# Half of the short convolution of two state-space stages moved from VectorE to GpSimd, and constant TensorE products moved within their openings

## The chip, the cores and the metric

The kernel runs on one NeuronCore of a Trainium2 chip (trn2). The metric is the device time of one launch in microseconds, as the median of several runs. Engines are called by their names in the profile: PE is TensorE, DVE is VectorE, ACT is ScalarE, POOL is GpSimd, SP is SyncE; PEld is TensorE loading weights.

## What is computed

The reference is a four-layer decoder with twelve sub-layers on x of shape (16, 128, 256). The change touches the fourth and the seventh, which are selective-state mixers (layer 1 with 4 heads and state 64, layer 2 with 32 heads and state 128). Cut to what matters:

```python
zxbcdt = layernorm(x) @ W_in              # z: 512, xBC: 512 + 2 * state, dt: heads
xt = pad(transpose(xBC), left=3)
xt = conv(xt, conv_w, depthwise, 4 taps)
xBC = silu(transpose(xt + conv_b))
dt = softplus(dt + dt_bias)
Y = scan(X * dt, -exp(A_log) * dt, B, C) + D * X
g = Y * silu(z)
x = x + (g * rsqrt(mean(g * g) + eps) * norm_w) @ W_out
```

## The kernel before, in words

Each sub-layer is one stage with a program written out by hand for every engine; semaphores (`Signal`) tie them together, and each engine runs its own list strictly in order. Both mixers are built by one function, `mixer`. In the trace the first one runs from about 442 to 648 us, the second from about 941 to 1229 us.

The 16 sequences are worked on one by one (index q, L2144 on), in 4 groups g of 4 sequences (T = 512 columns). A group first needs its projections: the normalised input is transposed ("turn"), split into a rounded part and a rest (`xh`, `xl`), and multiplied in three products. The 512 + 2 * state convolution channels are handled in six chunks c = 0..5 of 128 rows (chunks 4 and 5 have 64 rows in the first stage). For each chunk

- PE computes the projection into a PSUM bank ("conv" job, L262);
- ACT copies it into the padded buffer `cx` (L1735), which has two slots, c % 2, and writes the product with the last tap into `xc` (L1737); this function is `pad`, and it frees the PSUM bank;
- DVE adds the other three taps with three `scalar_tensor_tensor` of 128x512 in a chain (L1886, function `conv`), out = cx shifted * tap + out;
- ACT applies SiLU with the bias (L1751, function `silu`). All six chunks must have it before PE transposes rows of the next group (`rows`, L2073, which waits for `xc_ready`).

`pad` of chunk c waits for the convolution of chunk c - 2, since it reuses its slot. The gates z go the same way without a convolution: PE, then ACT's SiLU into `zs` (L1757, function `gate`).

The projections of group g + 1 are interleaved with the work on the four sequences of group g, by the position t = q % 4: at t = 0 chunks 0 and 1, at t = 1 chunks 2 and 3, at t = 2 chunks 4 and 5 and the step sums, at t = 3 the gates and all SiLUs (`first_part`, `middle_part`, `second_part`). "first" jobs stand ahead of the sequence's outputs, "second" ones behind them. These jobs take turns in two PSUM banks, freed in the order of use.

On a sequence q itself: ACT exponentiates the decays `e` (L1770), DVE weighs them (L1916, `weigh`, one instruction of 128x512 per sequence in the first stage, four of 128x1024 in the second), PE forms the outputs (L2106, then L2117 or L2113), DVE gates them (L1927, `gated`) and takes the next values (L1906 or L1903, `values`), ACT squares (L1776) and copies the similarity of the next sequence (L1763), POOL adds the squares in two steps (L1705, L1707, `add_squares`), PE projects out (L2128, L2130, `project_out`), which waits among others for the next similarity. The steps (L1852 to L1860), `split` (L1867, L1868) and `levels` (L1874, L1876) are small DVE work for the next group.

The opening of a stage does all jobs of group 0 in a row (list `FIRST`, eight PSUM banks): PE runs ahead; ACT's order is pad 0, softplus, pad 1, pad 2, some scaled copies, pad 3, more copies, pad 4, pad 5, a table load, four gates, six SiLUs. `idle_products(pe, k, bank, n)` (L245) issues n products of constants (128x512, f32, two rows of the trace each) whose result nobody reads: three when the stage begins, and three after every first job has been read, right ahead of the first exponents (L2088). On DVE the norm of group 1 is the last work of the opening; its POOL part adds epsilon and raises to the power (L210, L212).

## Time and profile before

| | |
|---|---|
| median of 3 runs | 2408.22 us (2404.01 to 2409.35) |
| profiled execution, its own time | 2404.21 us |
| its span, first to last instruction | 2402.4 us |
| PE busy in the span | 2116.3 us (88%) |
| DVE / ACT / POOL busy | 1585.9 (66%) / 1237.8 (52%) / 294.7 us (12%) |
| mean granted TensorE clock | 0.937 of full speed |

How to read the rows further down. A row of the windows gives the stretch in us from the span's start, its length, then for PE, PEld, DVE, ACT and POOL the busy time in it and the number of instructions, then the mean granted TensorE clock as a share of full speed, the DMA share and GB/s. A row of a timeline gives start, duration, engine, line, operation, out<-in by the program's names, the shapes, how many instructions were merged, and in brackets how long the engine had been idle and what released it. A row of a single line gives its instructions' shortest, median and longest duration in ns and the first and last start. A row of the waits gives who waited for whom, the total in us, how often, and the longest.

### The profile page before, as it was taken

To read this page: it belongs to the slowest core of one execution; us is meant where nothing else is said; L and a number is where in the kernel's file an instruction comes from. 1 tells how busy PE (TensorE), PEld (TensorE's weight loads), DVE (VectorE), ACT (ScalarE), POOL (GpSimd) and SP (SyncE) were. 2 spreads that over 40 slices of the span, in tenths; PEclk is the share of its full clock that TensorE was granted. 3 is DMA by queue.
4 is the path that set the end of the run, shared out by engine and by line. 5 is a ranking of instruction groups with operands and counts; after the bars stand their busy time and mean duration, and the time that the engine had idled before them with its cause. 6 is when DMAs were issued, how large, how long until landed. Compare 5 with 4: busy or idle time off the path is not lost. (4 is left out here: it accounts for less than half of the span.)

```text
span 2402.4 us, 46894 instructions
## 1 busy us (share of the span) xinstructions
PE 2116.3 (88%) x18960; PEld 1600.0 (67%) x18963; DVE 1585.9 (66%) x2975; ACT 1237.8 (52%) x2457; POOL 294.7 (12%) x301
## 2 busy tenths in 40 slices
PE   7979979899899898888889998957989879999996
PEld 5644437677655687566656666646656667999996
DVE  4433476666565897877848666787666676676663
ACT  3336714444466443655536446644467724566653
POOL 0010000010210000001000000000100111444342
PEclk9989989899999998999999999978989978999998
DMA  2020001100110002000010010010200024766673
GB/s 98 21 81 10 2 20 48 36 1 1 40 37 2 33 1 70 1 1 1 1 32 1 9 61 0 0 35 1 71 1 2 6 71 169 220 202 199 203 220 86
DMA packets 62649, 125.59 MB, mean 52 GB/s; under 512 B 16056, under 2 KB 45369, under 8 KB 62297
## 3 DMA queue, kind: packets, MB, share of 16 engines
q1 hardware_dynamic: 53626, 110.83, 13.5%
q0 software_dynamic: 8832, 12.06, 2.4%
q8 instruction: 138, 2.26, 0.4%
q14 instruction: 53, 0.43, 0.1%
HBM read 109.18 MB, written 15.80 MB: 52 GB/s over the span
## 5 line engine op out<-in xcount | busy, mean ns | idle before, releaser
L262 PE MATMUL ps<-ffn_xh,ffn_wh 128*128 128x256 f32 x644 | 184.0, 286 | 1.5 <-DVE ffn_xl L4228 1.5
L262 PE MATMUL ps<-ffn_xh,ffn_wl 128*128 128x256 f32 x644 | 182.2, 283 | 0.0
L262 PE MATMUL ps<-ffn_xl,ffn_wh 128*128 128x256 f32 x644 | 182.1, 283 | 0.0
L4223 DVE TENSOR_TENSOR ffn_wl<-ffn_fresh,ffn_wh 128x1792 fp32r<-128x1792 f32 x69 | 139.3, 2022 | 26.3 <-ACT ffn_wh L4101 26.2
L1886 DVE SCALAR_TENSOR_TENSOR attn_xc<-attn_cx,all_w,attn_xc 128x512 f32<-128x512 f32 (+1 forms) x144 | 107.3, 749 | 50.3 <-ACT attn_xc L1737 46.7
L210 POOL TENSOR_TENSOR all_rstd<-all_mv,all_cst 128x4 f32<-128x4 f32 x41 | 9.6, 233 | 1066.8 <-DVE all_mv L193 1066.7
L262 PEld LDWEIGHTS ps<-ffn_xh,ffn_wh 128*128 128x128 f32 x644 | 123.3, 192 | 1.7 <-DVE ffn_xl L4228 1.7
L4101 ACT ACTIVATE ffn_wh<-ffn_fresh 128x1792 fp32r<-128x1792 f32 x69 | 116.9, 1694 | 13.6 <-DMA ffn_fresh<-in_l3f_w 13.6
L262 PEld LDWEIGHTS ps<-ffn_xl,ffn_wh 128*128 128x128 f32 x644 | 123.4, 192 | 0.0
L262 PEld LDWEIGHTS ps<-ffn_xh,ffn_wl 128*128 128x128 f32 x644 | 123.3, 192 | 0.0
L2880 ACT ACTIVATE xattn_sc<-xattn_sc,xattn_mx 128x128 f32<-128x128 f32 x256 | 98.8, 391 | 17.7 <-DVE xattn_mx L2955 17.7
L1175 PE MATMUL ps<-ffn_xh,ffn_w 128*128 128x512 f32 x224 | 94.7, 423 | 13.3 <-ACT ffn_w L3147 11.2
L4088 POOL DMA_INDIRECT x_acc<-ffn_y,ffn_row_i x46 | 79.2, 1721 | 214.5 <-ACT ffn_y L4129 211.7
L248 PE MATMUL ps<-all_cst 128*128 128x512 f32 x114 | 70.0, 771 | 33.0 <-ACT attn_zs L1757 9.3
L1916 DVE TENSOR_TENSOR attn_e<-attn_e,all_w 128x1024 f32<-128x1024 f32 (+1 forms) x80 | 87.1, 1122 | 16.4 <-ACT attn_e L1770 15.1
L262 PE MATMUL ps<-ffn_wh,ffn_hh 128*128 128x256 f32 x322 | 94.1, 292 | 3.9 <-DVE ffn_hl L4236 3.9
L254 PE MATMUL ps<-all_xnT,all_w 128*128 128x512 f32 (+1 forms) x176 | 90.1, 644 | 4.2 <-ACT all_xnT L753 2.6
L1175 PE MATMUL ps<-ffn_xl,ffn_w 128*128 128x512 f32 x224 | 93.5, 417 | 0.0
L262 PE MATMUL ps<-ffn_wl,ffn_hh 128*128 128x256 f32 x322 | 91.0, 283 | 0.0
L262 PE MATMUL ps<-ffn_wh,ffn_hl 128*128 128x256 f32 x322 | 90.9, 282 | 0.0
L200 DVE TENSOR_SCALAR all_xn<-all_x,all_mv,all_rstd 128x256 f32<-128x256 f32 (+1 forms) x164 | 59.9, 428 | 38.2 <-POOL all_rstd L212 38.0
L4246 DVE TENSOR_TENSOR all_xnT<-ps,all_xn 128x512 f32<-128x512 f32 x92 | 57.1, 621 | 41.5 <-PE ps L262 38.4
(484 smaller groups left out, 6100.6 us busy)
## 6 DMA issues: line engine op xcount, KB each, us to landing
ffn_fresh<-in_l3f_w SPq DMA_DIRECT2D x69, 896.0 KB, 4.7
all_w<-in_ctxT SPq DMA_DIRECT2D x12, 512.0 KB, 6.1
all_w<-in_ctx SPq DMA_DIRECT2D x8, 512.0 KB, 6.3
all_x<-in_x_rows SPq DMA_DIRECT2D x4, 512.0 KB, 7.4
all_x<-x_seq SPq DMA_DIRECT2D x4, 512.0 KB, 5.3
all_w<-in_l2x_o SPq DMA_DIRECT2D x1, 2048.0 KB, 9.1
xattn_ctxT<-in_ctxT SPq DMA_DIRECT2D x4, 512.0 KB, 3.9
all_w<-in_l2f_up SPq DMA_DIRECT2D x1, 2048.0 KB, 9.1
```

Of the source, the lines that this page charges most:

```text
L200: dve.tensor_scalar(k.xn[:, t, :], k.x[:, i * TG + t, :], k.mv[:, t, 0:1], k.rstd[:, t, 0:1], ALU.subtract, ALU.mult).then_inc(self.xn_rea ...
L248: pe.matmul(k.psum[bank][:, :], k.c["ident"], k.cst[:, 0:512], start=True, stop=True)
L254: last = pe.matmul(out, w[:, c, n0:n1], k.xnT[:, c, a:b], start=start and c == 0, stop=stop and c == KC - 1)
L262: last = pe.matmul(out, a, b, start=start and n == 0, stop=stop and n == 2)
L1175: last = pe.matmul(out, w[:, c, f * P:(f + 1) * P], part[:, c, :], start=c == 0 and n == 0, stop=c == KC - 1 and n == 1)
L1886: ins = dve.scalar_tensor_tensor(out, cx[0:n, c % 2, :, j:j + P], tap, out, ALU.mult, ALU.add)
L1916: dve.tensor_tensor(e[:, d % SLOTS_E], e[:, d % SLOTS_E], gm[:, q % 2].unsqueeze(1).broadcast_to([P, HP, P]), ALU.mult).then_inc(m_ready.s ...
L2880: last = act.activation(s, s, ACT.Exp, bias=mx[:, n % nS, e, h:h + 1], scale=-1.0, accum_out=total[:, n % nS, e, h:h + 1])
L4088: pool.indirect_dma_start(acc[:, :], bass.IndirectOffsetOnAxis(ap=row_i[:, at:at + 1], axis=0), y[:, j % 2, v, :], None, compute_op=ALU.ad ...
L4101: act.activation(wh[:, j % 2, piece(q)], fresh[:, piece(q)], ACT.Copy).then_inc(high_ready.sem, 1)
L4223: dve.tensor_tensor(wl[:, j % 2, piece(q)], fresh[:, piece(q)], wh[:, j % 2, piece(q)].bitcast(F32), ALU.subtract).then_inc(low_ready.sem, 1)
L4246: dve.tensor_tensor(h[:, n % 2, 0:width], B[n % 2][:, 0:width], sa[:, n % 2, 0:width], ALU.mult).then_inc(h_ready.sem, 1)
```

## The change

Chunks 1, 3 and 5 are convolved on POOL instead of DVE, in both mixers and for all groups. POOL has no fused form here: each tap is a product (`tensor_scalar` with the tap, into a temporary) and a sum (`tensor_tensor`), each waiting for the one before. The temporary is a part of `zs` which the first gate of the group writes later, so from group 1 on that gate waits for the last odd chunk. `conv_ready` is split into one signal for even chunks (DVE) and one for odd ones (POOL). The norm of group 1 is split in DVE's opening. Of the constant products, those at the stage's start go ahead of the first convolution job (into bank 6), and those ahead of the exponents go, four instead of three, in front of the waits for the last banks.

```diff
@@ -1669,7 +1669,8 @@
     soft_ready = Signal(k, "soft_ready")
     steps_ready = Signal(k, "steps_ready")
     levels_ready = Signal(k, "levels_ready")
-    conv_ready = Signal(k, "conv_ready")
+    conv_ready = [Signal(k, f"conv_ready{e}") for e in range(2)]
+    conv_steps = Signal(k, "conv_steps")
     xc_ready = Signal(k, "xc_ready")
     g_psum = Signal(k, "g_psum")
     gm_ready = Signal(k, "gm_ready")
@@ -1686,8 +1687,18 @@
     x_added = Signal(k, "x_added")
     steps = Signal(k, "vector_steps")
 
+    EVEN = C // 2
+
     def cols(t):
         return slice(t * P, (t + 1) * P)
+
+    def convolved(g, c):
+        return conv_ready[c % 2](0, EVEN * g + c // 2 + 1)
+
+    def taps(g, c, j):
+        n = m.sizes[c]
+        return (xc[0:n, g % 2, c, :].rearrange("p (t l) -> p t l", t=TG), cx[0:n, c % 2, :, j:j + P],
+                v["taps"][0:n, c, j:j + 1])
 
     with nc.Block() as block:
         @block.sync
@@ -1706,12 +1717,37 @@
                 pool.wait_ge(*sq_half(0, q + 1))
                 pool.tensor_tensor(sq[:, 0, :], sq[:, 0, :], sq[:, 1, :], ALU.add).then_inc(sq_summed.sem, 1)
 
+            steps_done = [0]
+
+            def conv(g, c):
+                key = ("conv", g, c)
+                jobs(key).wait_freed(pool, key)
+                for j in range(TAPS - 1):
+                    out, source, tap = taps(g, c, j)
+                    tmp = zs[0:m.sizes[c], g % 2 if g else 1, 0, :].rearrange("p (t l) -> p t l", t=TG)
+                    pool.tensor_scalar(tmp, source, tap, None, ALU.mult).then_inc(conv_steps.sem, 1)
+                    steps_done[0] += 1
+                    pool.wait_ge(*conv_steps(0, steps_done[0]))
+                    ins = pool.tensor_tensor(out, out, tmp, ALU.add)
+                    if j < TAPS - 2:
+                        ins.then_inc(conv_steps.sem, 1)
+                        steps_done[0] += 1
+                        pool.wait_ge(*conv_steps(0, steps_done[0]))
+                    else:
+                        ins.then_inc(conv_ready[1].sem, 1)
+
             norm.pool(pool, 0)
+            conv(0, 1)
+            conv(0, 3)
             norm.pool(pool, 1)
+            conv(0, 5)
             for q in range(BATCH):
+                g, t = q // TG + 1, q % TG
                 add_squares(q)
-                if q % TG == 3 and q // TG + 2 <= last_group:
-                    norm.pool(pool, q // TG + 2)
+                if t < 3 and g <= last_group:
+                    conv(g, 2 * t + 1)
+                if t == 3 and g + 1 <= last_group:
+                    norm.pool(pool, g + 1)
 
         @block.scalar
         def _(act):
@@ -1731,7 +1767,7 @@
                 key, n = ("conv", g, c), m.sizes[c]
                 jobs(key).wait_full(act, key)
                 if g * C + c >= 2:
-                    act.wait_ge(*conv_ready(0, g * C + c - 1))
+                    act.wait_ge(*(convolved(g, c - 2) if c >= 2 else convolved(g - 1, c - 2 + C)))
                 act.activation(cx[0:n, c % 2, :, TAPS - 1:], jobs(key).bank(key)[0:n, :].rearrange("p (t l) -> p t l", t=TG),
                                ACT.Copy)
                 act.activation(xc[0:n, g % 2, c, :], jobs(key).bank(key)[0:n, :], ACT.Copy,
@@ -1747,13 +1783,15 @@
 
             def silu(g, c):
                 n = m.sizes[c]
-                act.wait_ge(*conv_ready(0, g * C + c + 1))
+                act.wait_ge(*convolved(g, c))
                 act.activation(xc[0:n, g % 2, c, :], xc[0:n, g % 2, c, :], ACT.Silu,
                                bias=v["conv_b"][0:n, c:c + 1]).then_inc(xc_ready.sem, 1)
 
             def gate(g, c):
                 key = ("gate", g, c)
                 jobs(key).wait_full(act, key)
+                if c == 0 and g >= 1:
+                    act.wait_ge(*convolved(g, C - 1))
                 act.activation(zs[:, g % 2, c, :], jobs(key).bank(key)[:, :], ACT.Silu).then_inc(jobs(key).freed(key), 1)
 
             def similarity(q):
@@ -1878,16 +1916,15 @@
                 last.then_inc(levels_ready.sem, 1)
 
             def conv(g, c):
-                key, n = ("conv", g, c), m.sizes[c]
+                key = ("conv", g, c)
                 jobs(key).wait_freed(dve, key)
-                out = xc[0:n, g % 2, c, :].rearrange("p (t l) -> p t l", t=TG)
                 for j in range(TAPS - 1):
-                    tap = v["taps"][0:n, c, j:j + 1]
-                    ins = dve.scalar_tensor_tensor(out, cx[0:n, c % 2, :, j:j + P], tap, out, ALU.mult, ALU.add)
+                    out, source, tap = taps(g, c, j)
+                    ins = dve.scalar_tensor_tensor(out, source, tap, out, ALU.mult, ALU.add)
                     if j < TAPS - 2:
                         chain(ins)
                     else:
-                        ins.then_inc(conv_ready.sem, 1)
+                        ins.then_inc(conv_ready[0].sem, 1)
 
             def values(q):
                 g, t = q // TG, q % TG
@@ -1959,17 +1996,15 @@
             dve.wait_ge(*rates_ready(0, 1))
             chain(dve.tensor_scalar(negA[:, :, :], negA[:, :, :], -1.0, None, ALU.mult))
             step_sizes(0)
-            conv(0, 1)
             conv(0, 2)
             for n in range(SETS):
                 split(0, n)
             levels(0, 0)
-            conv(0, 3)
+            norm.stats(dve, 1)
             if SETS > 1:
                 levels(0, 1)
             conv(0, 4)
-            conv(0, 5)
-            norm.vector(dve, 1)
+            norm.normalize(dve, 1)
             values(0)
             for q in range(BATCH):
                 g, t = q // TG + 1, q % TG
@@ -1979,7 +2014,7 @@
                     if q >= 1 and i == PU - 1:
                         add(q - 1)
                 for key in first_part(q):
-                    if key[0] == "conv":
+                    if key[0] == "conv" and key[2] % 2 == 0:
                         conv(*key[1:])
                     if key[0] == "turn":
                         rest(*key[1:])
@@ -1993,7 +2028,7 @@
                 if more and t == 1:
                     step_sizes(g)
                 for key in second_part(q):
-                    if key[0] == "conv":
+                    if key[0] == "conv" and key[2] % 2 == 0:
                         conv(*key[1:])
                 if more and t == 2:
                     for n in range(SETS):
@@ -2007,7 +2042,6 @@
 
         @block.tensor
         def _(pe):
-            idle_products(pe, k, 0, 3)
             pe.wait_ge(*own)
 
             def turn(g, u):
@@ -2131,11 +2165,14 @@
                           skip_group_check=True).then_inc(out_psum.sem, 1)
 
             for key in FIRST:
+                if key == ("conv", 0, 0):
+                    idle_products(pe, k, 6, 3)
                 JOBS[key[0]](*key[1:])
-            for key in FIRST[-len(first_jobs.banks):]:
+            for n, key in enumerate(FIRST[-len(first_jobs.banks):]):
                 first_jobs.wait_freed(pe, key)
+                if n == 0:
+                    idle_products(pe, k, (4, 5, 6, 7, 0, 1, 2, 3)[(len(FIRST) - 8) % 8], 4)
             pe.wait_ge(*padding_set(0, 1))
-            idle_products(pe, k, 0, 3)
             exponents(0)
             rows(0)
             pe.wait_ge(*scaled_ready(0, 1))
```

Where the order moves. On POOL, at the opening of the first mixer (L210 and L212 are the norm's steps, L1728 and L1731 of the change the product and the sum, L1705 and L1707 of before the squares). Before:

```order
L1701 TENSOR_SCALAR attn_before<-all_cst 128x128
L210 TENSOR_TENSOR all_rstd<-all_mv,all_cst 128x4
L212 TENSOR_TENSOR all_rstd<-all_rstd,all_cst 128x4
L210 TENSOR_TENSOR all_rstd<-all_mv,all_cst 128x4
L212 TENSOR_TENSOR all_rstd<-all_rstd,all_cst 128x4
L1705 TENSOR_TENSOR all_w<-all_w 128x256
L1707 TENSOR_TENSOR all_w<-all_w 128x128
```

In the change, at the end of the same opening (chunk 3's last tap, the norm of group 1, chunk 5, the first sequence's squares):

```order
L1728 TENSOR_SCALAR attn_zs<-attn_cx,all_w 128x512
L1731 TENSOR_TENSOR attn_xc<-attn_xc,attn_zs 128x512
L210 TENSOR_TENSOR all_rstd<-all_mv,all_cst 128x4
L212 TENSOR_TENSOR all_rstd<-all_rstd,all_cst 128x4
L1728 TENSOR_SCALAR attn_zs<-attn_cx,all_w 64x512
L1731 TENSOR_TENSOR attn_xc<-attn_xc,attn_zs 64x512
L1728 TENSOR_SCALAR attn_zs<-attn_cx,all_w 64x512
L1731 TENSOR_TENSOR attn_xc<-attn_xc,attn_zs 64x512
L1728 TENSOR_SCALAR attn_zs<-attn_cx,all_w 64x512
L1731 TENSOR_TENSOR attn_xc<-attn_xc,attn_zs 64x512
L1716 TENSOR_TENSOR all_w<-all_w 128x256
L1718 TENSOR_TENSOR all_w<-all_w 128x128
```

Six instructions per odd chunk now stand between the norm's and the squares' steps on POOL.

On DVE, at the end of the opening of the first mixer (L1876 or L1914 are the levels, L1886 or L1923 the convolution, L188 to L200 the norm of group 1, L1906 or L1943 the first values). Before:

```order
L1876 TENSOR_SCALAR attn_vm<-all_w,all_cst 32x512 x4
L1886 SCALAR_TENSOR_TENSOR attn_xc<-attn_cx,all_w,attn_xc 128x512 x3
L1886 SCALAR_TENSOR_TENSOR attn_xc<-attn_cx,all_w,attn_xc 64x512 x6
L188 BN_STATS all_bn<-all_x 128x6 x4
L191 MEMSET all_spare 128x1
L193 BN_AGGR all_mv<-all_bn 128x2 x4
L200 TENSOR_SCALAR all_xn<-all_x,all_mv,all_rstd 128x256 x4
L1906 TENSOR_TENSOR all_w<-ps,all_w 128x512
```

In the change:

```order
L1914 TENSOR_SCALAR attn_vm<-all_w,all_cst 32x512 x4
L188 BN_STATS all_bn<-all_x 128x6 x4
L191 MEMSET all_spare 128x1
L193 BN_AGGR all_mv<-all_bn 128x2 x4
L1923 SCALAR_TENSOR_TENSOR attn_xc<-attn_cx,all_w,attn_xc 64x512 x3
L200 TENSOR_SCALAR all_xn<-all_x,all_mv,all_rstd 128x256 x4
L1943 TENSOR_TENSOR all_w<-ps,all_w 128x512
```

Six of the nine convolution instructions are gone from this place, and the statistics stand ahead of chunk 4.

## Rows read from the trace of the kernel before

**Rows 1.** Windows: opening and rest of the first stage, rest of the second.
```profile
442.00:486.00 44.00, 36.13 (x130) 24.74 (x131) 29.42 (x65) 24.44 (x44) 5.16 (x7) 0.77 0.14 49
486.00:650.00 164.00, 154.28 (x829) 121.46 (x829) 104.69 (x192) 78.15 (x166) 22.21 (x37) 0.95 0.00 1
...
992.00:1230.00 238.00, 208.18 (x1968) 149.14 (x1966) 181.81 (x276) 128.45 (x212) 21.80 (x36) 0.96 0.01 2
```

**Rows 2.** Waits of the second stage after its opening (total us, times, longest).
```profile
PE ps L2113 <- DVE attn_e L1916: 19.5, 38, 0.9
```

**Rows 3.** Timelines of DVE, ACT and PE in both openings.
```profile
462.01 4.64 DVE L1886 SCALAR_TENSOR_TENSOR attn_xc<-attn_cx,all_w,attn_xc 128x512 f32<-128x512 f32 x6 [1.70 <-ACT attn_xc L1737]
...
472.97 0.59 ACT L1735 ACTIVATE attn_cx<-ps 64x512 f32<-64x512 f32 x1 [3.82 <-DVE attn_xc L1886]
477.37 3.78 ACT L1751 ACTIVATE attn_xc<-attn_xc,all_w 128x512 f32<-128x512 f32 x6
...
477.77 5.46 PE L248 MATMUL ps<-all_cst 128*128 128x512 f32 x6 [3.84 <-ACT attn_zs L1757]
483.81 0.66 PE L2073 MATMUL ps<-all_cst,attn_xc 128*128 128x128 f32 x4
...
986.08 0.66 PE L2073 MATMUL ps<-all_cst,attn_xc 128*128 128x128 f32 x4
```

**Rows 4.** Single lines: the convolution on VectorE, and GpSimd's nearest operations.
```profile
L1886 DVE SCALAR_TENSOR_TENSOR attn_xc<-attn_cx,all_w,attn_xc x144: 732/752/754, 454.3 to 1171.2; 128x512 f32<-128x512 f32 x120, 64x512 f32<-64x512 f32 x24
...
L1705 POOL TENSOR_TENSOR all_w<-all_w x32: 724/730/775, 489.6 to 1225.6; 128x256 f32<-128x256 f32 x32
...
L2247 POOL TENSOR_TENSOR xattn_sq<-all_w x4: 1892/1892/1893, 649.7 to 705.3; 128x1024 f32<-128x1024 f32 x4
...
L3706 POOL TENSOR_SCALAR xattn_neg<-xattn_allowed x4: 607/608/608, 1915.1 to 1929.5; 1x512 f32<-1x512 int32 x4
```

**Rows 5.** GpSimd and VectorE at the same time (timelines).
```profile
443.93 1.47 DVE L1946 TENSOR_TENSOR attn_win_low<-all_w,attn_win_high 128x1288 fp32r<-128x1288 f32 x1
444.10 1.36 POOL L210 TENSOR_TENSOR all_rstd<-all_mv,all_cst 128x4 f32<-128x4 f32 x1 [0.32 <-DVE all_mv L193]
...
552.86 0.73 POOL L1705 TENSOR_TENSOR all_w<-all_w 128x256 f32<-128x256 f32 x1 [15.50 <-ACT all_w L1776]
552.86 0.75 DVE L1852 SCALAR_TENSOR_TENSOR all_w<-all_w,attn_dtA 128x16 f32<-128x16 f32 x1 [0.15 <-DVE all_w L1906]
...
553.66 0.49 POOL L1707 TENSOR_TENSOR all_w<-all_w 128x128 f32<-128x128 f32 x1
```

**Rows 6.** Timelines in the first stage, second sequence: VectorE, ACT, PE.
```profile
497.54 2.33 DVE L1886 SCALAR_TENSOR_TENSOR attn_xc<-attn_cx,all_w,attn_xc 128x512 f32<-128x512 f32 x3 [0.23 <-ACT attn_xc L1737]
501.19 2.33 DVE L1886 SCALAR_TENSOR_TENSOR attn_xc<-attn_cx,all_w,attn_xc 128x512 f32<-128x512 f32 x3 [0.33 <-ACT attn_xc L1737]
...
504.69 0.26 ACT L1763 ACTIVATE all_w<-ps 128x128 f32<-128x128 f32 x1
...
505.05 1.97 PE L2128 MATMUL ps<-all_w,all_xnT 128*128 128x256 f32 x8
```

**Rows 7.** The same timelines, third and fourth sequence.
```profile
512.66 0.67 DVE L1906 TENSOR_TENSOR all_w<-ps,all_w 128x512 f32<-128x512 f32 x1
...
513.75 1.06 PE L2059 MATMUL ps<-all_cst,all_w 128*32 128x128 f32 x8
...
515.12 2.30 DVE L1886 SCALAR_TENSOR_TENSOR attn_xc<-attn_cx,all_w,attn_xc 64x512 f32<-64x512 f32 x3 [1.79 <-ACT attn_xc L1737]
...
518.70 0.60 ACT L1757 ACTIVATE attn_zs<-ps 128x512 f32<-128x512 f32 x1
...
525.52 0.66 PE L2073 MATMUL ps<-all_cst,attn_xc 128*128 128x128 f32 x4 [0.27 <-ACT attn_zs L1757]
```

**Rows 8.** Timeline of VectorE in the second stage, second sequence.
```profile
1002.14 4.57 DVE L1886 SCALAR_TENSOR_TENSOR attn_xc<-attn_cx,all_w,attn_xc 128x512 f32<-128x512 f32 x6 [2.40 <-ACT attn_xc L1737]
1006.62 2.35 DVE L1916 TENSOR_TENSOR attn_e<-attn_e,all_w 128x1024 f32<-128x1024 f32 x2
```

## The prediction

> **What bounds the kernel now.** I read the windows first, then the waits and the timelines of the two mixers. In the windows [rows 1] PE is busy 154.3 of the 164 us that follow the opening of the first mixer (94%), DVE 104.7 (64%). The second mixer is tighter between the two: PE 208.2 of 238 us (87%), DVE 181.8 (76%), and there PE's largest wait for work is the weighing by DVE, 19.5 us in 38 waits [rows 2]. The openings are bound by neither: in the first, PE works 36.1 of 44 us at a mean clock of 0.77. Its timeline shows what ends last [rows 3]: ACT waits 3.82 us for DVE's convolution before it can pad chunk 5 (472.97), its SiLUs end at 477.37 + 3.78 = 481.15, but PE transposes rows only at 483.81, since three constant products stand ahead, 5.46 us at the lower clock level. So 2.66 us of the first opening are lost to products. In the second opening the transposes start at 986.08 [rows 3], behind products of the same kind.
>
> **What DVE gets back.** Nine of 18 convolution instructions per group go, at 752 ns [rows 4], 2.3 us per odd chunk. In the first mixer that is worth nothing by itself: DVE has a third of its time free. What it hides is the price of delay, below.
>
> **What GpSimd takes for one odd chunk.** Its nearest rows [rows 4] are the sums of squares: 730 ns for 256 columns and 1892 ns for 1024; on the line between them 512 columns take 730 + 256 x 1.51 = 1.12 us. A product with a scalar on 512 columns exists in one row, on one partition: 608 ns. Bounds for the product: 0.6, and the sum's 1.12 above. I take 0.61, the row with the same column count. Between dependent POOL instructions lie 0.07 us (552.86 + 0.73 to 553.66 [rows 5]). Three taps: 3 x (0.61 + 1.12) + 5 x 0.07 = 5.5 us, against 2.3 on DVE; with the upper bound for the product 7.1.
>
> For the same price the Trainium skill's page GPSIMD Engine Reference, section Elementwise — side-by-side cycle accounting, has two figures: 512 elements of a one-input loop in 769 ns, and some 2.5 to 2.6 cycles per element at 1.2 GHz for two inputs, which is an estimated 1.25 us with a fixed part. By these a chunk would take about 6.4 us, and the sum below would be some 7 us higher. The rows put the product lower and the sum lower; no row has these exact forms.
>
> **What the two do to each other.** The rows show that they exclude each other on such operands [rows 5]. POOL's addition at 444.10 took 1.36 us and ended 0.06 us after DVE's subtraction (443.93 + 1.47 = 445.40); the second row of this kind, at 552.86, is DVE's turn to suffer: a 128x16 operation took 0.75 us and ended with POOL's 0.73. So whenever DVE's convolution or weighing meets POOL's, they alternate: a DVE operation waits up to 0.61 or 1.12 us. Three convolution instructions of DVE in a row that meet POOL's chunk take about 3.9 us and not 2.3, and POOL's chunk becomes 5.5 + 3 x 0.55 = 7.2 us (0.55 being the 0.75 less a start-up of 0.2 that passes while it waits; an estimate).
>
> **First mixer, one group.** *Second sequence* [rows 6]: chunk 1 is padded at 497.54, POOL starts there and is still at it when DVE begins chunk 2 at 501.19. Chunk 2 ends 1.5 us later. Behind it on DVE stand the gating, behind that ACT's square and the similarity, which ends at 504.95; PE projects out at 505.05, so there is 0.1 us of slack: +1.4 us. *Third sequence* [rows 7]: POOL is on chunk 3 while DVE does chunk 4, again some 1.6 to 2 us. Behind it stand the values of the fourth sequence (512.66 to 513.33), which free the PSUM bank for the step sums of PE (513.75): slack 0.4 us, so +1.9 with the earlier shift partly absorbed, 3.3 us in all. *Fourth sequence* [rows 7]: chunk 5 was ready on DVE at 515.12 + 2.30. POOL needs 5.5 us plus what the weighing and five level instructions take of it, about 7.1, and starts later by the shift of ACT (3.7): it ends about 515.1 + 3.7 + 7.1 = 525.9. The first gate now waits for it; it stood at 518.70. From the gate to PE's transposes it was 6.8 us (518.70 to 525.52); some 1.8 of it, waits for PE's later gates, should fall away when the first is late (an estimate), so the transposes move to about 530.9, +5.4 us. I take 5.0 us for a group, three groups (of the fourth there is nothing to prepare): **+15.0**. Ends: with no interference the chunk alone would end at 520.6 and cost about 0.5 us per group, 1.5 in all; with a slow product, 1.6 us more for each of the three chunks in part, 7.5 per group, 22.5 in all.
>
> **Second mixer, one group** [rows 8]. Chunks 0 and 1 took 4.57 us on DVE, and the weighing at 1006.62 stood behind them. It can now begin some 2 us earlier, but alternates with POOL: four weighings of 1.2 us against five POOL operations. The first two end up to 0.8 us earlier than before, the last two 0.4 and 1.0 us later, and PE, which waits for each, ends the sequence 1.0 us later. The same in the third sequence; in the fourth DVE is fed from PSUM while POOL does chunk 5, and PE wins back a part. I take +1.4 per group: **+4.2**. Ends: -2 per group (the released DVE time shortens the 19.5 us of waits by a third, no interference) and +4.
>
> **The openings.** POOL does chunks 1, 3, the norm of group 1, then chunk 5, in a row. ACT pads chunk 3 only after chunk 1 is done, chunk 5 after chunk 3. In the first mixer chunk 1 was padded at 462.0 [rows 3]; I take 461.5, since PE comes to it a little earlier. With interference 7 us each and 1.2 for padding give 469.7 for the start of chunk 3, 476.8 for its end; chunk 5's padding ends at 478.0 against 473.0 + 1.2 = 474.2. Table load and gates (474.2 to 477.4, 3.2 us) and SiLUs (3.8) follow: 485.0; on POOL itself the norm and chunk 5 end near 485, and the last SiLU behind it at 485.6. So transposes at about 485.6 instead of 483.81: +1.8. The removed 2.66 us of products are in that. The second mixer in the same way, with its two sets of levels on DVE in between: +2.0. Products run right behind the last gate projection now, near 471 to 475, and PE then idles for about 10 us with only the first exponents between. Before, it came out of the products at the upper clock level; the mean clock of the opening, 0.77 [rows 1], says that 20 of its 44 us ran at the lower. I expect the transposes and the first outputs at the lower level. If 5 us of PE work so take twice the time and part is covered by ACT and DVE: +2.5 in the first mixer, +1.5 in the second. The three products ahead of the first convolution job start where PE waits for the rest, and run past that wait; I cost them at nothing, since DVE's weight rest and ACT's copies lie beside them, and PE makes up the time at a higher clock before chunk 1. Without that cover they would cost up to 2 us in each opening. Openings together: 1.8 + 2.0 + 2.5 + 1.5 = **+7.8**. Ends: -6 (POOL fast, products gone from the path in both) and +14.
>
> **Sum.** 15.0 + 4.2 + 7.8 = +27 on the profiled execution's 2404.2 us, which gives 2431.2. The median of the runs shown, 2408.2, lies 4 us above that execution, and the forecast is for a median: 2435.
>
> **The rivals.**
> *A, faster.* GpSimd and DVE hardly meet, the chunk takes 5.5 us beside other work, and what is left are the gains: 2.7 us of products in the first opening, 3 in the second, 2 us of DVE waits for each of three groups of the second mixer: 6 + 5.7 = -12, a median of 2397. For it speaks that POOL was busy only 22 of 164 us [rows 1]. Against it speak rows 5 and the 0.1 us of slack. It decides by whether DVE's convolution instructions stay at 752 ns. The Trainium skill's page SBUF — State Buffer, section Who interferes with whom, says of this that a DVE instruction with two SBUF inputs contends with a GpSimd instruction that reads SBUF, and the later one is fully blocked; by that rule A is out.
> *B, no change.* The interference is there, but slacks I have not seen take it up: 1.5 us per group in the first mixer, nothing in the second, openings even. +4.5 against a gain of up to 5 from products: 2405 to 2412.
> *C, slower still.* The product costs what the sum costs, 7.1 us alone and 9 with interference. Each group of the first mixer 7.5, of the second 3, openings +14: +45, 2453.
> *D, the idle PE.* The chain costs as in B, but the low clock after 10 idle us holds through the first sequences of both mixers: +10 in all, 2418.
>
> **How the numbers follow.** Forecast (POOL's port and latency bind, 2418 to 2448) 0.50; C 0.10; D 0.13; B 0.14; A 0.13. A measurement of this kernel can tell about 0.2%, 4.8 us, from no change. C, D and the forecast are slower: 0.73; B is the same: 0.14; A is faster: 0.13. The range, 2403 to 2450, leaves out A and the upper half of C. The likeliest case's own range is 2418 to 2448.
>
> **What would show it.** DVE's convolution instructions at a mean over 0.9 us where they were 0.752; POOL's product near 0.6 and sum near 1.1 at the shortest, much longer at the median; a wait of ACT for POOL before the first gate of groups 1 to 3 in the first mixer; PE waiting for SiLU about 5 us longer per group there; transposes of the openings 2 us later, at the lower clock. The forecast falls if the convolution instructions are not stretched, if the first gate does not wait in the first mixer, or if the windows of the first mixer's groups are not longer by more than 2 us each.

## The result, and the profile after

| | median, us | executions | ratio to before, 95% interval |
|---|---|---|---|
| before, on the same chip | 2408.78 (2404.01 to 2410.68) | 4 | |
| after | 2476.34 (2473.26 to 2481.35) | 4 | 1.0286 [1.0269, 1.0304] |

The change costs 67.6 us where 27 were forecast. The direction was right, the size was out of the range (2403 to 2450) and above the dearest rival, C, with its 2453. The profiled execution after has a span of 2474.8 us, 72.4 more than before.

A clock of its own shows where it went: the time from the start of a stage (the first memset of the padded buffer, 442.16 and 940.95 us before, 446.37 and 988.26 after) to GpSimd's first addition of the squares of its first, 13th and 16th sequence. Up to the first is the opening, from there to the 13th are the three groups that prepare a next one.

| | before: first, 13th, 16th | after | opening | three groups | forecast for the two |
|---|---|---|---|---|---|
| first mixer | 47.4, 187.6, 204.5 | 59.2, 234.3, 251.2 | +11.8 | +34.9 | +4.3, +15.0 |
| second mixer | 55.9, 255.1, 284.6 | 65.2, 282.9, 312.1 | +9.3 | +18.5 | +3.5, +4.2 |

The line of the profile page on VectorE's even chunks (busy us and mean ns behind the first bar):

```profile
L1923 DVE SCALAR_TENSOR_TENSOR attn_xc<-attn_cx,all_w,attn_xc 128x512 f32<-128x512 f32 (+1 forms) x72 | 71.0, 987 | 45.6 <-ACT attn_xc L1773 43.9
```

GpSimd's product and sum and the same line of VectorE as single lines (shortest, median, longest ns), to be held against [rows 4]:

```profile
L1728 POOL TENSOR_SCALAR attn_zs<-attn_cx,all_w x72: 1556/1756/3673, 465.5 to 1247.7; 128x512 f32<-128x512 f32 x60, 64x512 f32<-64x512 f32 x12
L1731 POOL TENSOR_TENSOR attn_xc<-attn_xc,attn_zs x72: 1252/1278/1857, 467.1 to 1251.3; 128x512 f32<-128x512 f32 x60, 64x512 f32<-64x512 f32 x12
L1923 DVE SCALAR_TENSOR_TENSOR attn_xc<-attn_cx,all_w,attn_xc x72: 739/753/1794, 459.9 to 1233.5; 128x512 f32<-128x512 f32 x60, 64x512 f32<-64x512 f32 x12
```

The product takes 1.56 us at the shortest, not 0.61; the sum 1.25, not 1.12. A chunk alone takes 3 x (1.56 + 1.26) + 0.5 = 9.0 us, not 5.5. VectorE's instruction has kept its median and gained a tail: a mean of 987 ns where it was 749.

**The opening of the first mixer**, timelines of POOL, ACT and PE. POOL's rows are the first and last of chunk 1 (465.47), of chunk 3 (476.46), then the norm's steps and the ends of chunk 5:

```profile
465.47 1.57 POOL L1728 TENSOR_SCALAR attn_zs<-attn_cx,all_w 128x512 f32<-128x512 f32 x1 [14.68 <-ACT attn_xc L1773]
...
473.76 1.34 POOL L1731 TENSOR_TENSOR attn_xc<-attn_xc,attn_zs 128x512 f32<-128x512 f32 x1
476.46 1.56 POOL L1728 TENSOR_SCALAR attn_zs<-attn_cx,all_w 128x512 f32<-128x512 f32 x1 [1.36 <-ACT attn_xc L1773]
...
484.65 1.26 POOL L1731 TENSOR_TENSOR attn_xc<-attn_xc,attn_zs 128x512 f32<-128x512 f32 x1
485.87 0.20 POOL L210 TENSOR_TENSOR all_rstd<-all_mv,all_cst 128x4 f32<-128x4 f32 x1
486.15 1.04 POOL L212 TENSOR_TENSOR all_rstd<-all_rstd,all_cst 128x4 f32<-128x4 f32 x1
487.26 1.77 POOL L1728 TENSOR_SCALAR attn_zs<-attn_cx,all_w 64x512 f32<-64x512 f32 x1
...
495.11 1.25 POOL L1731 TENSOR_TENSOR attn_xc<-attn_xc,attn_zs 64x512 f32<-64x512 f32 x1
```
```profile
475.19 0.60 ACT L1771 ACTIVATE attn_cx<-ps 128x512 f32<-128x512 f32 x1 [7.17 <-POOL attn_xc L1731]
486.00 0.59 ACT L1771 ACTIVATE attn_cx<-ps 64x512 f32<-64x512 f32 x1 [7.43 <-POOL attn_xc L1731]
496.40 0.72 ACT L1787 ACTIVATE attn_xc<-attn_xc,all_w 64x512 f32<-64x512 f32 x1 [2.83 <-POOL attn_xc L1731]
490.79 0.59 PE L2122 MATMUL ps<-attn_before,all_identb 128*128 128x512 bf16 x1 [10.68 <-ACT attn_zs L1795]
...
497.17 1.12 PE L2107 MATMUL ps<-all_cst,attn_xc 128*128 128x128 f32 x4 [5.08 <-ACT attn_xc L1787]
...
500.71 1.92 PE L2140 MATMUL ps<-attn_xc,all_w 128*128 128x128 f32 x8
```

GpSimd works from 465.5 to 496.4 with one pause, the 1.36 us in which ACT pads chunk 3. ACT's waits for it before chunk 3 and before chunk 5 take the place of the 3.82 us in [rows 3], and the last SiLU waits once more. The transposes start 50.8 us into the stage; before, at 483.81, it was 41.65. Four transposes take 1.12 us where [rows 3] had 0.66: the lower clock level, after PE had waited 10.68 us before the exponents and 5.08 us behind them.

**A group of the first mixer**, around its fourth sequence; POOL's first and last row of chunk 5, then ACT's gate, PE's gate projections and transposes:

```profile
538.60 1.56 POOL L1728 TENSOR_SCALAR attn_zs<-attn_cx,all_w 64x512 f32<-64x512 f32 x1
...
546.50 1.25 POOL L1731 TENSOR_TENSOR attn_xc<-attn_xc,attn_zs 64x512 f32<-64x512 f32 x1
547.83 1.28 ACT L1795 ACT_TABLE_LOAD   x1 [7.34 <-POOL attn_xc L1731]
549.78 0.79 PE L262 MATMUL ps<-attn_xh,attn_win_high 128*128 128x512 f32 x1 [5.14 <-ACT attn_zs L1795]
550.37 0.63 PE L262 MATMUL ps<-attn_xl,attn_win_high 128*128 128x512 f32 x1
...
554.98 0.60 PE L2107 MATMUL ps<-all_cst,attn_xc 128*128 128x128 f32 x4
```

This is the wait that was foreseen: ACT 7.34 us for GpSimd, and behind ACT's gate, which frees a PSUM bank, PE. After that idle time PE's projections run at 0.63 us, against 0.40 at the upper level.

**The windows from the first to the 13th square** (the three groups), first mixer then second mixer, of before:

```profile
489.60:629.70 140.10, 132.70 (x699) 103.88 (x698) 93.31 (x174) 70.46 (x146) 17.16 (x28) 0.94 0.00 1
996.90:1196.10 199.20, 174.70 (x1559) 125.98 (x1558) 158.19 (x246) 110.36 (x182) 17.02 (x29) 0.95 0.00 1
```

and of after:

```profile
505.60:680.60 175.00, 141.19 (x701) 110.32 (x700) 91.49 (x147) 70.87 (x146) 101.11 (x82) 0.87 0.00 1
1053.50:1271.20 217.70, 181.06 (x1565) 130.48 (x1564) 166.63 (x219) 110.00 (x182) 119.14 (x83) 0.93 0.00 1
```

VectorE, the fifth figure with its count, executes 27 instructions fewer in either mixer, worth 27 x 0.75 = 20 us. Yet its busy time falls by only 1.8 us in the first and rises by 8.4 in the second. What was taken off it came back as longer instructions. In the second mixer the 27 that stayed take 28.3 us, 8 more than at 0.75 us each, and the 48 weighings 15.5 us more. Their windows before and after:

```profile
996.90:1196.10 199.20, 56.47 (x48) 0.95 0.00 1
```
```profile
1053.50:1271.20 217.70, 71.99 (x48) 0.93 0.00 1
```

In the first mixer the 27 take 24.8 us, 4.6 more, and the 12 levels 12.6 us instead of 5.7. PE is also busy for 8.5 and 6.4 us longer, at a lower clock. Its largest waits after, two of the first mixer and one of the second:

```profile
PE ps L262 <- ACT attn_zs L1795: 18.1, 3, 6.8
PE ps L2164 <- POOL all_w L1718: 6.7, 4, 2.4
```
```profile
PE ps L2147 <- DVE attn_e L1953: 14.1, 19, 1.6
```

In the second mixer the wait for the weighing is 14.1 us, against 16.4 in the same window before: nearly nothing of the relief has arrived. How it is lost shows in the timelines of the second sequence there, to be held against [rows 8]; POOL, then DVE:

```profile
1062.66 3.16 POOL L1728 TENSOR_SCALAR attn_zs<-attn_cx,all_w 128x512 f32<-128x512 f32 x1 [7.88 <-ACT attn_xc L1773]
...
1067.28 3.47 POOL L1728 TENSOR_SCALAR attn_zs<-attn_cx,all_w 128x512 f32<-128x512 f32 x1
```
```profile
1063.25 2.77 DVE L1953 TENSOR_TENSOR attn_e<-attn_e,all_w 128x1024 f32<-128x1024 f32 x2
1066.34 3.06 DVE L1953 TENSOR_TENSOR attn_e<-attn_e,all_w 128x1024 f32<-128x1024 f32 x2
1069.32 3.56 DVE L1923 SCALAR_TENSOR_TENSOR attn_xc<-attn_cx,all_w,attn_xc 128x512 f32<-128x512 f32 x3
```

Two weighings take 2.8 and 3.1 us instead of 2.35, three convolutions 3.6 instead of 2.3, and GpSimd's product 3.2 to 3.5 instead of 1.56.

### The profile page after: what moved, and what is told of

Read it like the earlier page. It is cut to its first block and busy times, and to the rows that moved or that the text cites. A ratio compares the mean times of both kernels' runs of the same rounds, so it can differ in the third digit from the quotient of the medians.

```text
span 2474.8 us, 46980 instructions
## 1 busy us (share of the span) xinstructions
PE 2118.8 (86%) x18964; PEld 1603.9 (65%) x18967; DVE 1592.2 (64%) x2903; ACT 1238.1 (50%) x2457; POOL 535.6 (22%) x445
## 5 line engine op out<-in xcount | busy, mean ns | idle before, releaser
L210 POOL TENSOR_TENSOR all_rstd<-all_mv,all_cst 128x4 f32<-128x4 f32 x41 | 10.0, 244 | 992.6 <-DVE all_mv L193 992.6
L1728 POOL TENSOR_SCALAR attn_zs<-attn_cx,all_w 128x512 f32<-128x512 f32 (+1 forms) x72 | 141.2, 1962 | 90.0 <-ACT attn_xc L1773 84.8
L1953 DVE TENSOR_TENSOR attn_e<-attn_e,all_w 128x1024 f32<-128x1024 f32 (+1 forms) x80 | 104.6, 1340 | 18.8 <-ACT attn_e L1808 17.5
L1175 PE MATMUL ps<-ffn_xh,ffn_w 128*128 128x512 f32 x224 | 93.3, 416 | 13.1 <-ACT ffn_w L3184 11.4
L1923 DVE SCALAR_TENSOR_TENSOR attn_xc<-attn_cx,all_w,attn_xc 128x512 f32<-128x512 f32 (+1 forms) x72 | 71.0, 987 | 45.6 <-ACT attn_xc L1773 43.9
L1731 POOL TENSOR_TENSOR attn_xc<-attn_xc,attn_zs 128x512 f32<-128x512 f32 (+1 forms) x72 | 97.9, 1359 | 6.0
L262 PE MATMUL ps<-attn_xh,attn_win_high 128*128 128x512 f32 (+1 forms) x160 | 75.9, 474 | 22.2 <-ACT attn_zs L1795 21.6
```

Source lines behind the costliest of these rows:

```text
L262: last = pe.matmul(out, a, b, start=start and n == 0, stop=stop and n == 2)
L1175: last = pe.matmul(out, w[:, c, f * P:(f + 1) * P], part[:, c, :], start=c == 0 and n == 0, stop=c == KC - 1 and n == 1)
L1728: pool.tensor_scalar(tmp, source, tap, None, ALU.mult).then_inc(conv_steps.sem, 1)
L1731: ins = pool.tensor_tensor(out, out, tmp, ALU.add)
L1923: ins = dve.scalar_tensor_tensor(out, source, tap, out, ALU.mult, ALU.add)
L1953: dve.tensor_tensor(e[:, d % SLOTS_E], e[:, d % SLOTS_E], gm[:, q % 2].unsqueeze(1).broadcast_to([P, HP, P]), ALU.mult).then_inc(m_ready.s ...
```

## The experiments

Two theories. **Length**: GpSimd's chain is so slow that others wait for its end. **Interference**: it holds up VectorE's instructions, whoever waits for whom. A third question is what the moved constant products do. All times are medians with the ratio to before on the same chip; "stages" are the 16th squares on the clock above (before: 204.5 and 284.6). Single profiled stages of the same code differ by up to 5.3 us between runs (first mixer 199.8 to 205.1 in three kernels), so smaller differences of stages are not read. Everything outside of the two stages is the same code in all kernels and took 1905 to 1924 us in the profiled executions; a sum of stages and a difference of medians therefore agree only within some 10 us.

### The parts: products alone, convolution alone

The kernel before with only the constant products moved (these lines, the old two calls gone):

```diff
+                if key == ("conv", 0, 0):
+                    idle_products(pe, k, 6, 3)
...
+                if n == 0:
+                    idle_products(pe, k, (4, 5, 6, 7, 0, 1, 2, 3)[(len(FIRST) - 8) % 8], 4)
```

> The kernel before with only TensorE's constant products moved; the convolution stays on VectorE. If their place ahead of the exponents cost the 2.7 us that the first opening showed and the second as much: 2403 us. If the lower clock that an idle PE then has costs more than they save: over 2412. If both cancel: within 5 us of 2408.

Measured: 2404.94 us, 0.9986 [0.9973, 0.9999]. Stages 200.6 and 285.2. The lower clock shows here too: the four transposes of the first opening take 1.12 us after waits of 2.54 and 2.64 us, and the 12.5 us from there on have a granted clock of 0.78. Still the two openings are 1.1 and 1.4 us shorter than before.

The change with the products left in their old places (the same lines taken out of it):

> The change with the constant products left where they were before. If the 67 us are GpSimd's convolution alone: 2476, within 5 us, since the products can run while GpSimd is on chunk 5. If the moved products have a share in the loss, the time falls below 2470.

Measured: 2464.78 us, 1.0243 [1.0225, 1.0261]. Stages 247.1 and 304.6. The convolution costs 57.6 us. The moved products gain 2.2 us in the kernel before (on the edge of what can be told) and cost 11.6 in the change: they are no independent term.

### Which of the moved products

The change with the products at the stage's start where it has them, and those ahead of the exponents back behind the waits:

```diff
-            for n, key in enumerate(FIRST[-len(first_jobs.banks):]):
+            for key in FIRST[-len(first_jobs.banks):]:
                 first_jobs.wait_freed(pe, key)
-                if n == 0:
-                    idle_products(pe, k, (4, 5, 6, 7, 0, 1, 2, 3)[(len(FIRST) - 8) % 8], 4)
             pe.wait_ge(*padding_set(0, 1))
+            idle_products(pe, k, 0, 3)
```

> The change with the constant products at the stage's start where it has them (ahead of the first convolution job), but those ahead of the exponents back in their old place, three of them behind the waits. The whole change gave 2476.3, the change with both sets of products as before 2464.8. Theory 1 (what costs is the second set: ahead of the waits they leave the engine idle for over 10 us before the exponents when the convolutions are slow): 2463 to 2467, like the change with both as before, and the first squares of the stages at 56 and 63 us. Theory 2 (the first set costs, since it stands on the path to the projections): 2474 to 2478. Theory 3 (half each): 2469 to 2472.

Measured: 2460.58 us (2457 to 2469), 1.0219 [1.0199, 1.0239]: close to the 2464.78 with both sets in their old places, from which the intervals do not tell it. First squares at 56.9 and 63.8 us. So it is the second set. PE's timeline in the first opening:

```profile
486.02 5.46 PE L248 MATMUL ps<-all_cst 128*128 128x512 f32 x6 [15.63 <-ACT attn_zs L1795]
...
492.40 0.66 PE L2107 MATMUL ps<-all_cst,attn_xc 128*128 128x128 f32 x4
494.40 1.06 PE L2140 MATMUL ps<-attn_xc,all_w 128*128 128x128 f32 x8
```

Here the products lie beside ACT's SiLUs, the last of which ends at 492.35, and cost next to nothing. The transposes behind them take 0.66 us and the outputs 1.06, where the change has 1.12 and 1.92. The windows of the 12.5 or 12.8 us from the transposes on, of this kernel and of the change, with granted clocks of 1.00 and 0.63:

```profile
492.40:504.90 12.50, 12.50 (x82) 10.66 (x82) 5.44 (x9) 6.62 (x12) 1.19 (x2) 1.00 0.00 1
```
```profile
497.20:510.00 12.80, 12.80 (x64) 11.39 (x65) 4.23 (x7) 4.57 (x8) 1.19 (x2) 0.63 0.00 0
```

### The product made cheaper

A constant in the tap's place (the odd chunks are then multiplied by 0.25, so the values are others), and the product as an operation on two tensors with the tap broadcast:

```diff
-                    pool.tensor_scalar(tmp, source, tap, None, ALU.mult).then_inc(conv_steps.sem, 1)
+                    pool.tensor_scalar(tmp, source, 0.25, None, ALU.mult).then_inc(conv_steps.sem, 1)
```
```diff
+                    pool.tensor_tensor(tmp, source, tap.unsqueeze(2).broadcast_to([m.sizes[c], TG, P]), ALU.mult).then_inc(conv_steps.sem, 1)
```

> The change with the tap of GpSimd's product replaced by the constant 0.25, so the odd chunks' convolution uses one number for all channels. If it is the per-partition operand that makes the product take 1.6 us, it falls to about 0.6 and the whole to about 2435, the sum of the prediction. If the product is slow on 128 partitions whatever its scalar is: product 1.56 us and 2476.

Measured: 2471.91 us, 1.0259 [1.0238, 1.0279], which the intervals do not tell from the change.

> The change with GpSimd's product as tensor_tensor, the tap broadcast along the row. If a two-input operation of 512 columns costs the 1.25 us of the sum, each tap is 0.3 us shorter, a chunk 1 us; with some 15 chunks of 24 on the path that is 2461. If the time is interference with VectorE and not length, two inputs make it no shorter: 2476.

Measured: 2463.23 us, 1.0234 [1.0212, 1.0257]. The products of the first, then product, sum and VectorE's convolution of the second:

```profile
L1728 POOL TENSOR_SCALAR attn_zs<-attn_cx x72: 1481/1589/2352, 464.6 to 1246.9; 128x512 f32<-128x512 f32 x60, 64x512 f32<-64x512 f32 x12
```
```profile
L1728 POOL TENSOR_TENSOR attn_zs<-attn_cx,all_w x72: 1029/1246/2076, 460.3 to 1234.0; 128x512 f32<-128x512 f32 x60, 64x512 f32<-64x512 f32 x12
L1731 POOL TENSOR_TENSOR attn_xc<-attn_xc,attn_zs x72: 1252/1592/2164, 461.4 to 1236.0; 128x512 f32<-128x512 f32 x60, 64x512 f32<-64x512 f32 x12
L1923 DVE SCALAR_TENSOR_TENSOR attn_xc<-attn_cx,all_w,attn_xc x72: 745/1203/1759, 454.7 to 1223.0; 128x512 f32<-128x512 f32 x60, 64x512 f32<-64x512 f32 x12
```

Nearly none of the price is in reading the tap: with a constant the product is still 1.48 us at the shortest. As a two-tensor operation the product falls to 1.03 us, which would save 1.6 us a chunk, but the sum's median rises from 1.28 to 1.59 and VectorE's from 0.75 to 1.20: a part of what a shorter chain gives is taken back by instructions that hold each other up. By stages (234.9, 315.4, against 251.2, 312.1) it helps in the first mixer, by 16.3 us, and not in the second.

### Length without interference, interference without length

Length alone: product and sum replaced by memsets of the same duration into space that nobody reads then (the odd chunks keep only their last tap, and so leave out three quarters of the convolution):

```diff
-                    pool.tensor_scalar(tmp, source, tap, None, ALU.mult).then_inc(conv_steps.sem, 1)
+                    pool.memset(side[:, 0:1750], 0.0).then_inc(conv_steps.sem, 1)
...
-                    ins = pool.tensor_tensor(out, out, tmp, ALU.add)
+                    ins = pool.memset(side[:, 0:1390], 0.0)
```

> The change with GpSimd's products and sums replaced by memsets of about the same length that read nothing, so the odd chunks keep only their last tap. If the length of the chain costs: at least three quarters of the 67 us stay, 2458 or above. If interference costs: VectorE's instructions keep 0.75 us and the time falls below 2440.

Measured: 2434.44 us, 1.0128 [1.0102, 1.0153]. Stages 242.5 and 279.7. The memsets, VectorE's convolution, its levels, and the window of the second mixer's three groups:

```profile
L1728 POOL MEMSET attn_zs<- x72: 1554/1560/1725, 460.2 to 1206.6; 128x1750 f32 x72
L1923 DVE SCALAR_TENSOR_TENSOR attn_xc<-attn_cx,all_w,attn_xc x72: 739/751/754, 454.6 to 1195.6; 128x512 f32<-128x512 f32 x60, 64x512 f32<-64x512 f32 x12
L1914 DVE TENSOR_SCALAR attn_vm<-all_w,all_cst x48: 521/610/1866, 466.2 to 1220.2; 128x512 fp32r<-128x512 f32 x32, 32x512 fp32r<-32x512 f32 x16
...
1040.50:1228.00 187.50, 168.29 (x1559) 125.47 (x1558) 140.28 (x219) 109.47 (x182) 93.09 (x83) 0.96 0.01 1
```

Of the first mixer's 46.7 us this keeps 38.0, and of the two openings' 11.8 and 9.3 us it keeps 9.8 and 7.2. In the second mixer, 27.5 lost become 4.9 gained, and the groups alone go from 199.2 to 187.5. VectorE is busy 140.3 us there, 17.9 less than before; with real operands it was 166.6. So interference costs VectorE 26 us in these groups, and the length is harmless there. PE's wait for the weighing falls to 2.7 us in seven waits.

The memsets are not free of interference everywhere. In the first mixer's groups the 12 levels take 19.7 us, more than in the change (12.6), and VectorE is as busy as before. They are not what PE waits for: its largest wait there is the one behind the gate, as in the change (18.1 us), and none is for the levels.

```profile
PE ps L262 <- ACT attn_zs L1795: 19.3, 3, 6.6
```

Interference alone: the kernel before, with GpSimd doing the same chain on rows of its own at the same places, in the first mixer only; nobody waits for it, and VectorE still does all chunks.

```diff
+                for j in range(TAPS - 1):
+                    pool.tensor_scalar(side[0:n, 1, :], side[0:n, 0, :], v["taps"][0:n, c, j:j + 1], None,
+                                       ALU.mult).then_inc(side_steps.sem, 1)
...
+                    pool.tensor_tensor(side[0:n, 2, :], side[0:n, 2, :], side[0:n, 1, :], ALU.add).then_inc(side_steps.sem, 1)
```

> The kernel before, all convolutions on VectorE, and in the first mixer GpSimd besides does the same products and sums on private rows at the places of the change; nobody waits for them, only its own squares and norms stand behind them. If interference on the operands is what costs: the first mixer grows by 20 us or more of the 46.7 it grew in the change, 2430 or above. If the length of GpSimd's chain is what costs: the convolution instructions stretch, but the whole grows by under 10 us, 2409 to 2418.

Measured: 2427.26 us (2420 to 2433), 1.0093 [1.0062, 1.0123], between the two expected ranges. First mixer 221.3, +16.8, of which 6.7 in the opening and 10.1 in the groups; the second unchanged (284.5). VectorE's 144 convolution instructions rose from a mean of 749 to 878 ns, all of it in the first mixer: 72.0 us for its 72, 53.6 for the other 72. PE's wait for the weighing in the three groups, 0.4 us before, is 11.5 in six waits. So interference alone costs there too, with VectorE fully loaded. It doesn't simply add to the length: 38.0 and 16.8 make more than 46.7, and in the change PE has no such wait in these groups.

### Where: opening or groups

The change in groups 1 to 3 only, and in the opening only, both with the constant products as before:

```diff
+    def on_pool(g, c):
+        return g >= 1 and c % 2 == 1
```
```diff
+    def on_pool(g, c):
+        return g == 0 and c % 2 == 1
```

> Odd chunks of groups 1 to 3 on GpSimd; the opening and the constant products as before. By the places of the squares in the change's trace, the groups hold 34.9 us in the first mixer and 18.5 in the second: 2408 + 53 = 2461. If part of that is a low clock handed on from the opening, it falls to 2445 or less.

Measured: 2461.35 us, 1.0229 [1.0212, 1.0246]. Stages 237.2 and 299.4.

> Odd chunks of group 0 alone on GpSimd, constant products as before. By the squares of the run with the products left in place, the openings hold 8.5 and 7.3 us: 2424. If the products, now behind GpSimd's chain, add to the path: 2430 or above.

Measured: 2424.49 us, 1.0065 [1.004, 1.0089]. Stages 214.6 and 294.4. By stages, +47.5 for the groups and +19.9 for the openings; with both at once, products also as before, 62.6. By medians they are 53.4, 16.5 and 57.6.

### One chunk less

The change with chunk 5 of groups 1 to 3 back on VectorE:

```diff
+    def on_pool(g, c):
+        return c in (1, 3) or (c == 5 and g == 0)
```

> The change with chunk 5 of groups 1 to 3 back on VectorE, in both mixers (chunks 1 and 3 stay on GpSimd; the opening is the change's). Theory 1 (in the first mixer the loss of a group is the chunk that the first gate waits for, 9 us where VectorE took 2.3): the 34.9 us that the three groups of the first mixer lost against the kernel before shrink by 15 to 20 us; in the second mixer, where interference costs, by a third of 18.5, some 6 us; about 2452. Rival (the loss is spread evenly over the three chunks, 1.3 us each per tap): a third of 34.9 and of 18.5 comes back, some 18 us in all, of it 11.6 in the first mixer, 2458; chunk 1's and chunk 3's delays keep the rest. Second rival (what comes late is ACT's work behind chunks 1 and 3, and chunk 5 hides behind it): under 5 us in the first mixer, 2468 or more.

Measured: 2457.9 us, 1.0217 [1.0198, 1.0236], 18.4 less than the change. In the first mixer the three groups take 157.8 us instead of 175.0: 17.3 of 34.9, half of the loss for a third of the chunks, while in the openings nothing changed. ACT's waits before the first gate fall from 24.7 us (three) to 3.4. The other half stays: chunks 1 and 3 still hold ACT before chunks 3 and 5, and PE's projection waits for GpSimd's squares, which queue behind them:

```profile
ACT attn_cx L1778 <- POOL attn_xc L1736: 8.9, 5, 2.3
PE ps L2171 <- POOL all_w L1723: 5.8, 5, 2.4
```

The second mixer's groups gained 11.8 us, twice what was expected for a third of the interference. The median of 2458 is the value of the even-spread rival and not the first theory's 2452, so it is the first mixer's stage that speaks for the gate (17.3 us, expected 15 to 20, the rival 11.6), and not the median.

### Two versions meant to keep the gain

The kernel before with the constant products moved, and in the second mixer, groups 1 to 3, first only chunk 5 on GpSimd (two-tensor product), then all odd chunks with their products on ACT and only the sums on GpSimd:

```diff
+    def on_pool(g, c):
+        return PADDED and g >= 1 and c == 5
```
```diff
+                        last = act.activation(zs[0:n, g % 2, j, :].rearrange("p (t l) -> p t l", t=TG), source, ACT.Copy,
+                                              scale=tap)
```

> The kernel before with both sets of constant products moved as in the change, and on GpSimd only chunk 5 of groups 1 to 3 of the second mixer, its product as a two-tensor operation with the tap broadcast (1.03 us at the shortest against 1.56). VectorE gives up 27 instructions of 0.75 us, 9 chunks' taps, in the group's third sequence. The kernel before with the products moved alone gave 2404.9. Theory (one chunk has a whole sequence of some 15 us for its 7 us, so only interference with the fourth sequence's work of VectorE counts, about 0.7 us per group, against 2.3 us per group of time returned to VectorE of which a third reaches PE): 2403 to 2407, no difference from 2404.9. Rival (relief counts: with length alone and no interference the groups of the second mixer took 12 us less for 9 chunks, so a third of that comes back): 2400 to 2402. Second rival (interference counts per chunk, 18.5 us for 9 chunks): 2410 to 2412.

Measured: 2406.12 us, 0.9998 [0.9985, 1.001]. The groups took 207.5 us, against 201.2 with the products alone moved, a little more than single stages can differ by. The expectation miscounts: chunk 5 of three groups is three chunks, and VectorE gives up 9 instructions and not 27 (135 of its 144 are left in the trace). Its ranges reckon with three of nine chunks and stand. The median lies in the first theory's, while the groups' 6.3 us are what the second rival had; the profiled execution is the slowest of the twelve.

> The kernel before with both sets of constant products moved as in the change, and in groups 1 to 3 of the second mixer the odd chunks with their three products on ACT (three Copy instructions with the tap as scale, about 0.6 us each, 16 us in all for nine chunks) and only the three sums on GpSimd (1.25 us each). GpSimd's chunk is 4 us instead of 9. Theory 1 (interference grows with the time that GpSimd's two-input operations overlap VectorE's, and half of it goes with the products): the groups lose 18.5 / 2 less the relief, and ACT's 1.8 us per chunk lie partly on the path: 2405 to 2412. Theory 2 (relief of VectorE wins once the chain is short, as with length alone, -12 us for the groups): 2395 to 2401. Theory 3 (each sum blocks VectorE as long as before, and ACT's additions are on the path): 2415 or more.

Measured: 2403.58 us, 0.999 [0.998, 0.9999], between the ranges of the first two theories. GpSimd's sums, and the window of the groups:

```profile
L1737 POOL TENSOR_TENSOR attn_xc<-attn_xc,attn_zs x27: 1270/2137/2257, 998.1 to 1171.1; 128x512 f32<-128x512 f32 x27
...
987.00:1191.70 204.70, 173.66 (x1565) 126.03 (x1564) 158.19 (x219) 126.42 (x209) 69.78 (x55) 0.96 0.00 1
```

VectorE gives up 27 instructions and is busy for 158.19 us, what it was before (158.19) and with the products alone moved (158.28): three sums of a chunk take back what three fused taps had cost. Neither version is better than the moved products alone (0.9986), and none of the three is further from the kernel before than 0.2%.

## Why the prediction was right or wrong

**Right.** What bounds the kernel, the direction, and nearly the price of GpSimd's sum (1.12 us for 1.25). The gate that waits for GpSimd in the first mixer, the mutual hold-up of GpSimd and VectorE, the waits for chunks 3 and 5 in the opening, and the low clock behind the emptied place of the constant products are all in the profile where they were foreseen. The clock terms fit: from the transposes to the addition of the first squares it takes 8.4 us in the change and 6.0 with the second set in its old place, 2.4 us (forecast 2.5), and 12.3 against 11.1, 1.2 us, in the second opening (forecast 1.5).

**Wrong: the price of the product.** This is the step that failed: "I take 0.61, the row with the same column count". It measured 1.56 us at the shortest, outside its upper bound of 1.12. The row (L3706) had the same columns but one partition and an integer input. It was the only row with 512 columns, but not the nearest one: in the kernel before, GpSimd's timeline has the same operation, a product with a scalar, on 128x128 elements:

```profile
443.23 0.55 POOL L1701 TENSOR_SCALAR attn_before<-all_cst 128x128 bf16<-128x128 f32 x1
```

That is 0.55 us for 128 columns on 128 partitions. With the 0.20 us of a 128x4 operation (485.87 above) as the fixed part and the rest scaled with the columns, 512 give 0.2 + 0.35 x 4 = 1.6 us. A chunk is 9.0 us alone, and 9.1 to 9.6 in the opening. With interference I had 7. Even rival C, named as the case of a dear product, had 7.1 alone. The price is not all of the miss: the run with the product at 1.03 us (the two-tensor form) still lost 56 us, with the gain in the first mixer alone. The Trainium skill's page GPSIMD Engine Reference (section Elementwise — side-by-side cycle accounting), by whose figures I estimated a chunk at 6.4 us, was too low as well: the 1.25 us estimated from its two-input figure is what the sum measured, 1.252, but its 769 ns for 512 elements of a tight loop is half of this product.

**Wrong: openings, +21.1 for +7.8.** Chunk 1 started 19.1 us into the stage (forecast 19.3). It took 9.6 us for 7, chunk 3 9.45 for 7.1, norm and chunk 5 together 10.5 for 8.2: 7.3 us more on the path, and the transposes came 50.8 us into the stage instead of 43.4. With SiLUs that late the constant products were off the path in their old place too (the run with the second set back shows them beside ACT's wait), so moving them took nothing off it and left only the price of the clock. The runs agree on the cause: memsets of the same length keep 17.0 of these 21.1 us.

**Wrong: groups of the first mixer, +34.9 for +15.0.** On the clock that starts with the first square, the forecast had chunk 5 on GpSimd from 29.2 to 36.3 us (525.9 less 489.6) and transposes at 41.3. In the change it ran from 33.0 to 42.2 and they came at 49.4; before, 35.9. So of 8.1 us too few, 3.8 are a later start (two slow chunks ahead of it), 2.1 the chunk's own length, and 2.2 that the way from gate to transposes did not shorten by 1.8 as estimated: a table load and projections at the lower clock stand in it. The run with memsets shows the mechanism: 38.0 of 46.7 us stay with the length alone, and the gate's wait with them. Chunk 5's return gives half of the groups' loss back, and with it the waits at the gate (24.7 to 3.4 us). The levels shrink back in that run too, but no wait of PE is for them. The lower bound for a group, that the chain might nearly fit, rested on the same product price.

**Wrong: groups of the second mixer, +18.5 for +4.2.** The mechanism was named (weighing alternates with GpSimd) and undersized. A single hold came out within the 1.1 us I had: weighings took up to 1.09 us longer, convolution instructions up to 1.04. But GpSimd's nine chunks took 9.8 to 13.1 us each in these groups and not 7.2, so they stood beside more of VectorE's instructions, and I had assumed that the relief of 2 us remained. Measured, the relief exists without interference (-11.7 us for three groups), and interference takes 26 us of VectorE's time. What would show it stood in the prediction, a mean over 0.9 us for the convolution: it was 0.987. The weighings, which the prediction named too, took more of the time (15.5 us) than the convolution (8 us). The Trainium skill's page SBUF — State Buffer (section Who interferes with whom) agrees with the runs in both directions: VectorE's convolution, with two inputs in SBUF, was stretched to 1.8 us by GpSimd's reading operations, and not at all (754 ns at most) by operations that only write.

**The rival A**, faster, needed a chunk of 5.5 us and VectorE's instructions at 752 ns; neither held. Its gain from the products exists in the kernel before (2.2 us of the forecast 5.7) and turns into a loss behind a slow chain.

**Left open.** Of 11.6 us between the change and its version without them, 5.3 lie in the openings; the rest is behind them (6.3 us by the stages of those two runs), whose code is the same, and single stages differ by 5.3 us. Whether the lower clock carries on into them was not separated. Why GpSimd's product costs more than its sum, no run shows.

## What to carry to other kernels

Moving elementwise work from VectorE to GpSimd gains nothing here even where VectorE is waited for: split into a product and a sum that both read SBUF, it gives back in stretched instructions what it takes off, and the only relief that reached PE was that of operations with no reads, which do not compute the result. Price such a move by the row of the same operation with all 128 partitions, scaled by columns (here an estimate of 1.6 us for 1.56), and not by the row that has the right column count but one partition and another type (0.61). Then test the length by a write-only stand-in and the interference by an idle copy of the chain, since here the two cost in different stages. And constant products that keep a clock up belong directly ahead of the work that needs it: moved in front of the waits they gained 2.2 us where the waits were 2.5 us long, and cost 11.6 where one was 10.7.
